# Decoder on one core: weights, last norm and memory products between the first experts and the second self attention

## What is computed

```python
def _L0_ffn_ref(x, w_router, w_gate, w_up, w_down, ..., shared_w_gate, shared_w_up, shared_w_down):
    probs = softmax(xt @ w_router)                     # 128 experts, the 4 best
    basis = silu((xt @ w_gate).reshape(T, 8, 256)) * (xt @ w_up).reshape(T, 8, 256)
    ...
    shared = silu(xt @ shared_w_gate) * (xt @ shared_w_up) @ shared_w_down
    return out + shared
def _L1_attn_ref(x, Wq, Wk, Wv, memory, memory_norm, memory_weight):
    q, k, v = x @ Wq.T, x @ Wk.T, x @ Wv.T             # 4 queries x 8 heads x 16
    probs = softmax(einsum('bsqhd,bthd->bqhst', qh, kh) * 0.25)
    a_dot = einsum('bqhst,bthd->bsqhd', probs, vh)
    sigma_q = elu(q.reshape(b, s, 4, 128))
    a_mem = sigma_q @ memory / (sigma_q @ memory_norm)
    w = sigmoid(memory_weight)
    return a_dot * (1 - w) + a_mem * w
...
x = layernorm(x + _L0_ffn_ref(x, ...))                 # third of six such steps
x = layernorm(x + _L1_attn_ref(x, ...))                # fourth
```

## Time and profile before

| what | us |
|---|---|
| median of 3 runs | 2482.82 |
| the three runs | 2481.49, 2482.82, 2499.75 |
| the execution that was profiled | 2499.76 |
| its span, first to last instruction | 2496.9 |
| end of the basis tiles to end of the experts' output products | 1427 to 1622 |
| PE idle between the experts and the first projection | 18.11 |
| self attention, from its first turn to its last product | 1623 to 1990 |

### The profile page before, as it was taken

How to read it: one execution, slowest core, us unless ns; L and a number is a source line. 1 busy time by engine, 2 the same in 40 slices (tenths; PEclk the granted TensorE clock), 3 DMA queues, 4 the chain that set the end, 5 groups by cost and what they waited for, 6 DMA issues and landing times. The chain is left out here.

```text
span 2496.9 us, 36997 instructions
## 1 busy us (share of the span) xinstructions
PE 2163.4 (87%) x13655; PEld 1731.6 (69%) x13669; DVE 1256.4 (50%) x3242; ACT 997.4 (40%) x2273; POOL 684.8 (27%) x627
## 2 busy tenths in 40 slices
PE   7999999999997889689999999858989748888774
PEld 6789889889875666568888777746555337766542
DVE  2654554553565666551111123246777546676646
ACT  3322232232235666431111111135656527777632
POOL 2732342332311111114343300035444222232110
PEclk9999999999996666899999999968999969999886
DMA  4210010100002100101000000033323030000001
GB/s 138 91 35 30 22 35 30 28 32 22 22 1 74 38 27 1 56 9 51 34 34 17 1 1 1 1 65 60 54 46 60 9 118 14 27 14 10 1 9 67
DMA packets 41297, 86.43 MB, mean 35 GB/s; under 512 B 6176, under 2 KB 20768, under 8 KB 38176
## 3 DMA queue, kind: packets, MB, share of 16 engines
q1 hardware_dynamic: 41120, 84.08, 12.0%
HBM read 63.55 MB, written 4.26 MB: 27 GB/s over the span
## 5 line engine op out<-in xcount | busy, mean ns | idle before, releaser
L1123 PE MATMUL PS<-WH,bXH 128*128 128x512 f32 x512 | 201.6, 394 | 5.4 <-POOL WL L1400 5.4
L1123 PE MATMUL PS<-WL,bXH 128*128 128x512 f32 x512 | 201.0, 393 | 0.0
L1123 PE MATMUL PS<-WH,bXL 128*128 128x512 f32 x512 | 200.9, 392 | 0.0
L1805 DVE TENSOR_REDUCE aM<-PS 128x4 f32<-128x1024 f32 x128 | 155.1, 1222 | 49.8 <-PE PS L1645 48.8
L1318 DVE SCALAR_TENSOR_TENSOR s<-s,cf,PS 128x256 f32<-128x256 f32 x112 | 53.9, 481 | 250.5 <-ACT s L1238 241.5
L1238 ACT ACTIVATE s<-PS 128x256 f32<-128x256 f32 x128 | 49.3, 385 | 280.1 <-PE PS L1123 280.1
L1748 ACT ACTIVATE aPT<-PS 128x1024 f32<-128x1024 f32 x128 | 129.5, 1024 | 70.2 <-PE PS L1665 69.2
L307 PE MATMUL PS<-aXH,QKH 128*128 128x512 f32 x384 | 154.0, 401 | 0.0
L307 PE MATMUL PS<-aXH,QKL 128*128 128x512 f32 x384 | 151.7, 395 | 0.0
L307 PE MATMUL PS<-aXL,QKH 128*128 128x512 f32 x384 | 151.5, 395 | 0.0
L506 ACT ACTIVATE sq<-PS 128x768 f32<-128x768 f32 x64 | 52.0, 812 | 209.0 <-PE PS L397 163.4
(11 more groups left out here) (400 smaller groups left out, 6161.0 us busy)
## 6 DMA issues: line engine op xcount, KB each, us to landing
lgB<-gate_sums SPq DMA_DIRECT2D x32, 256.0 KB, 3.7
sg<-in_gu SPq DMA_DIRECT2D x8, 1024.0 KB, 4.7
aqs<-aQH SPq DMA_DIRECT2D x64, 128.0 KB, 4.2
gQK<-in_Wqk SPq DMA_DIRECT2D x8, 768.0 KB, 5.9
xN<-in_xT SPq DMA_DIRECT2D x4, 1024.0 KB, 12.0
gC<-in_Wc SPq DMA_DIRECT2D x8, 512.0 KB, 4.9
xN<-in_x SPq DMA_DIRECT2D x4, 1024.0 KB, 7.1
cst<-in_cT SPq DMA_DIRECT2D x8, 512.0 KB, 4.7
```

The lines of the kernel that those rows point to most:

```text
L1123: mm = e.matmul(PS[:, b, :], x[:, kc, 128 * t:128 * t + 128], w[:, kc, :], start=kc == 0 and i == 0, stop=kc == KC - 1 and i == 2)
L1805: e.tensor_reduce(M[j % 2][:, :, :].rearrange("x q (h c) -> x h q c", h=2)[:, :, :, i], PS[:, b:b + 2, :].rearrange("p h (q k) -> p h q k" ...
```

## The change

In `experts0`: weight 9 is split in four chunks of its 512 rows, high half on ACT, low half on DVE in place of POOL, and PE waits chunk by chunk. Norms 0 to 2 are parted: statistics and seed after tiles 3, 7, 11; the other Newton rounds, the hand-over and ACT's part after tiles 4, 8, 12. Norm 3 leaves the stage.

In `attention1`: SP loads `aw` once weights 8 and 9 are split; the buffers are laid out in another order, so that `wst` lies where `sg` was. ACT splits to `WH` once PE has made the last shared products (`projected`), POOL in place of DVE splits to `WL`. `ks` is set to ones whole, one instruction for each buffer. The gates become a step `gate` at slot -27, norm 3 the steps `late1` to `late4` at slots -25 to -22. The step `memory` goes from 17 slots ahead of 8j to 11 for even j, from 22 to 18 for odd j.

```diff
@@ -1064,8 +1064,9 @@
+    up_hi, up_lo = K.flag("act_first_hi", KC), K.flag("dve_first_lo", KC)
...
-    w_hi, w_lo = K.flag("act_w_hi", 10), K.flag("pool_w_lo", 10)
+    w_hi, w_lo = K.flag("act_w_hi", 9), K.flag("pool_w_lo", 9)
@@ -1184,10 +1185,13 @@
             for a, k in ((0, 8), (1, 9)):
-                if t == 0:
+                if t == 0 and a == 0:
                     e.wait_ge(*w_hi.upto(k + 1))
...
                 for kc in range(KC):
+                    if t == 0 and a:
+                        e.wait_ge(*up_hi.upto(kc + 1))
+                        e.wait_ge(*up_lo.upto(kc + 1))
                     for i, (x, w) in enumerate(pair3((XH, WH[k % 2]), (XL, WL[k % 2]))):
@@ -1270,7 +1274,12 @@
                 silu(NT * k + t)
-            split_w(k + 2)
+            if k < 7:
+                split_w(k + 2)
+        e.wait_ge(*in_w[1].upto(5))
+        e.wait_ge(*t_mm.upto(8 * NT))
+        for kc in range(KC):
+            e.activation(WH[1][:, kc, :], sg[1][:, kc, :], ACTF.Copy).then_inc(up_hi.sem, 1)
@@ -1289,8 +1298,8 @@
                 shared(t + 1)
-            if t % 4 == 3:
-                norms[t // 4].apply_act(e)
+            if t >= 4 and t % 4 == 0:
+                norms[t // 4 - 1].apply_act(e)
@@ -1364,6 +1373,10 @@
             tile(n)
+        for kc in range(KC):
+            e.wait_ge(*up_hi.upto(kc + 1))
+            e.tensor_tensor(WL[1][:, kc, :], sg[1][:, kc, :], WH[1][:, kc, :].bitcast(F32),
+                            ALU.subtract).then_inc(up_lo.sem, 1)
@@ -1388,8 +1401,12 @@
             e.tensor_tensor(xN[:, t, :], PS[:, rooms["out", t][0], :], xN[:, t, :], ALU.add).then_inc(o_add.sem, 1)
-            if t % 4 == 3:
-                norms[t // 4].all_dve(e, step)
+            if t % 4 == 3 and t + 1 < NT:
+                norms[t // 4].stats(e, step)
+                norms[t // 4].seed(e, step)
+            elif t >= 4 and t % 4 == 0:
+                norms[t // 4 - 1].newton(e, step)
+                norms[t // 4 - 1].hand_over(e)
@@ -1440,7 +1458,8 @@
-    K.ends = (o_mm.upto(NT), u_hi.upto(2 * NT), o_add.upto(NT), t_add.upto(7 * NT), w_lo.upto(10))
+    K.late, K.loadable, K.projected = norms[NP - 1], (w_lo.upto(9), up_lo.upto(KC)), (h_mm.upto(NT),)
+    K.ends = (o_mm.upto(NT), u_hi.upto(2 * NT), o_add.upto(NT), t_add.upto(7 * NT), w_lo.upto(9), up_lo.upto(KC))
@@ -1451,11 +1470,10 @@
-    ends, came = K.ends, list(K.tx)
+    ends, came, late, loadable, projected = K.ends, list(K.tx), K.late, K.loadable, K.projected
...
-        PT = W("aPT", [128, 8, 2, 512])
@@ -1463,16 +1481,17 @@
+        M = [W(f"aM{i}", [128, 2, 16]) for i in range(2)]
+        rc, rm = W("arc", [128, 2, 16, 1]), W("arm", [128, 2, 2, 1])
+        mw, w1, w0 = W("amw", [128, 1]), W("aw1", [128, 1]), W("aw0", [128, 1])
+        mem = W("mem", [128, 130])
+        PT = W("aPT", [128, 8, 2, 512])
...
-        M = [W(f"aM{i}", [128, 2, 16]) for i in range(2)]
...
-        rc, rm = W("arc", [128, 2, 16, 1]), W("arm", [128, 2, 2, 1])
-        mem = W("mem", [128, 130])
-        mw, w1, w0 = W("amw", [128, 1]), W("aw1", [128, 1]), W("aw0", [128, 1])
@@ -1485,8 +1504,8 @@
         for lead, what, i in (((28, "turn_hi", 0), (27, "turn_lo", 0), (26, "key", 0), (25, "value", 0), (24, "query", 0),
-                               (23, "value_turn", 0), (22, "query", 1), (20, "elu", 0), (17, "memory", 0)) if j % 2 == 0 else
-                              ((28, "query", 0), (26, "query", 1), (24, "elu", 0), (22, "memory", 0))):
+                               (23, "value_turn", 0), (22, "query", 1), (20, "elu", 0), (11, "memory", 0)) if j % 2 == 0 else
+                              ((28, "query", 0), (26, "query", 1), (24, "elu", 0), (18, "memory", 0))):
             put(base - lead, 6, what, j, i)
@@ -1496,15 +1515,18 @@
+    put(-27, 7, "gate", 0)
+    for i, what in enumerate(("late1", "late2", "late3", "late4")):
+        put(-25 + i, 7, what, 0)
...
-    w_hi, w_lo = K.flag("act_w_hi", 11), K.flag("dve_w_lo", 11)
+    w_hi, w_lo = K.flag("act_w_hi", 11), K.flag("pool_w_lo", 11)
...
-    cleared, ones = K.flag("pool_cleared", 6), K.flag("pool_ones", 6)
+    cleared, ones = K.flag("pool_cleared", 6), K.flag("pool_ones", 3)
@@ -1690,13 +1712,13 @@
     def scalar(e):
-        for w in ends:
+        for w in projected:
             e.wait_ge(*w)
...
             e.activation(part(WH, m, h), source(m, h), ACTF.Copy).then_inc(w_hi.sem, 1)
-        e.wait_ge(*in_mw.upto(1))
-        e.activation(w1[:, :], mw[:, :], ACTF.Exp, scale=-1.0).then_inc(g_exp.sem, 1)
+        for w in ends:
+            e.wait_ge(*w)
         for what, j, i in plan:
@@ -1731,6 +1753,11 @@
                              ACTF.Identity, scale=w0[:, 0:1]).then_inc(v_out.sem, 1)
+            elif what == "gate":
+                e.wait_ge(*in_mw.upto(1))
+                e.activation(w1[:, :], mw[:, :], ACTF.Exp, scale=-1.0).then_inc(g_exp.sem, 1)
+            elif what == "late4":
+                late.apply_act(e)
             elif what == "elu":
@@ -1757,17 +1784,6 @@
         step = K.steps(e, "dve_step")
-        e.wait_ge(*in_w.upto(1))
-        for n, (m, h) in enumerate(blocks):
-            e.wait_ge(*w_hi.upto(n + 1))
-            e.tensor_tensor(part(WL, m, h), source(m, h), part(WH, m, h).bitcast(F32), ALU.subtract).then_inc(w_lo.sem, 1)
-        e.wait_ge(*g_exp.upto(1))
-        step(e.tensor_scalar(w1[:, :], w1[:, :], 1.0, None, ALU.add))
-        e.reciprocal(w1[:, :], w1[:, :]).then_inc(g_out.sem, 1)
-        e.wait_ge(*g_out.upto(1))
-        e.tensor_scalar(w0[:, :], w1[:, :], -1.0, 1.0, ALU.mult, ALU.add).then_inc(g_out.sem, 1)
-        e.wait_ge(*in_mem.upto(3))
-        e.tensor_scalar(mem[:, 0:128], mem[:, 0:128], w1[:, 0:1], None, ALU.mult).then_inc(g_out.sem, 1)
         for what, j, i in plan:
@@ -1777,6 +1793,22 @@
                                 XH[x][:, :, :].bitcast(F32), ALU.subtract).then_inc(x_lo.sem, 1)
+            elif what == "gate":
+                e.wait_ge(*g_exp.upto(1))
+                step(e.tensor_scalar(w1[:, :], w1[:, :], 1.0, None, ALU.add))
+                e.reciprocal(w1[:, :], w1[:, :]).then_inc(g_out.sem, 1)
+                e.wait_ge(*g_out.upto(1))
+                e.tensor_scalar(w0[:, :], w1[:, :], -1.0, 1.0, ALU.mult, ALU.add).then_inc(g_out.sem, 1)
+                e.wait_ge(*in_mem.upto(3))
+                e.tensor_scalar(mem[:, 0:128], mem[:, 0:128], w1[:, 0:1], None, ALU.mult).then_inc(g_out.sem, 1)
+            elif what == "late1":
+                late.stats(e, step)
+            elif what == "late2":
+                late.seed(e, step)
+            elif what == "late3":
+                late.newton(e, step)
+            elif what == "late4":
+                late.hand_over(e)
             elif what == "key":
@@ -1833,16 +1865,23 @@
     def gpsimd(e):
+        for w in projected:
+            e.wait_ge(*w)
+        for n, (m, h) in enumerate(blocks):
+            e.wait_ge(*w_hi.upto(n + 1))
+            e.tensor_tensor(part(WL, m, h), source(m, h), part(WH, m, h).bitcast(F32), ALU.subtract).then_inc(w_lo.sem, 1)
         for w in ends:
             e.wait_ge(*w)
-        for y in range(3):
-            for h in (0, 1):
-                e.memset(ks[y][64 * h + 32:64 * h + 64, :, :].bitcast(F32), 1.0).then_inc(ones.sem, 1)
-                e.wait_ge(*ones.upto(2 * y + h + 1))
+
+        def clear(y):
+            e.memset(ks[y][:, :, :].bitcast(F32), 1.0).then_inc(ones.sem, 1)
             e.memset(V[y][:, :, :, 16:32], 0.0).then_inc(cleared.sem, 1)
...
             e.wait_ge(*cleared.upto(2 * y + 2))
+
+        for y in range(3):
+            clear(y)
         for what, j, i in plan:
@@ -1874,9 +1913,11 @@
     def sync(e):
+        for w in loadable:
+            e.wait_ge(*w)
+        e.dma_start(wst[:, :, :], d["aw"]).then_inc(in_w.sem, 16)
         for w in ends:
             e.wait_ge(*w)
-        e.dma_start(wst[:, :, :], d["aw"]).then_inc(in_w.sem, 16)
         e.dma_start(mw[:, :], d["memw"].rearrange("(a n) -> a n", a=1).broadcast_to([128, 1])).then_inc(in_mw.sem, 16)
@@ -1889,7 +1930,7 @@
-                    e.wait_ge(*ones.upto(2 * y + 2))
+                    e.wait_ge(*ones.upto(y + 1))
```

## The result

The changed kernel takes 2428.12 us (median of 4 runs, 2418.93 to 2448.20), the kernel before 2491.28 in the same measurement (4 runs, with the earlier ones, 2481.49 to 2507.09): ratio 0.9755, 95% interval 0.9712 to 0.9798, some 61 us less. The profiled execution has a span of 2431.2 us, against 2496.9.

What follows compares the result with a forecast made beforehand. TensorE was taken to bound the stages, the gain being its idle time and the low clock after holes. Terms -7 - 19 - 15.6 - 6 - 10 = -57.6 us took 2482.82 to 2425 us; range 2407 to 2451.

Steps and rivals of the forecast that it cites:

- Part 1: Experts stage, shared expert: splitting the last weight in chunks removes PE's 4.29 us hole and the slow matmuls after it, -7 us.
- Part 2: Experts stage: parting norms 0 to 2 shortens PE's waits before the output products to 0.7 us and avoids low clock, -19 us.
- rival 2: Norms and prologue: short waits still cost the clock, -11 in place of -19 and 5 us more; 2438 us, chance 0.12.
- Part 3: Handover to the self attention: early weights, splits beside matmuls and a later last norm bring the key product forward, -15.6 us.
- Rival 4: Handover: the earlier start does nothing, as gate's DMA or POOL's splits hold PE as long; 2447 us, chance 0.06.
- Part 4: Self attention's prologue: scores 0 no longer wait behind both memory products; second key product 21.6 us earlier, 6 from this part.
- Part 5: Self attention's steady part: moved memory products avoid waits for POOL's `sgm`, -1.8 us a period, taken as -10, ends -20 and +15.
- Rival 1: Steady part: DVE becomes the bound in slots 5 to 7, +15 in place of -10; 2450 us, chance 0.12.
- Rival 3: Self attention falls to the low clock, as four cross attention slices at 0.6 suggest; up to 2585 us, chance 0.04.
- The rule of the Trainium skill: Prologue: DVE's two-port mode and POOL exclude each other; late norm's two tensor-scalars could wait, making the sum 3 us smaller.

Runs made afterwards that it cites:

- e1: Changed kernel with the last shared weight split whole again, high half on ACT, low half on POOL; first turn of the self attention 6.1 us later.
- e3: Changed kernel with the load of the attention's weights issued at the end of the experts stage again; turn to key product 15.4 us against 3.7.
- e4: Changed kernel with the norm of group 3 whole at the end of the experts stage again; turn to key product 16.2 us against 3.7.
- e5: Changed kernel with the memory products back at their old slots, 17 (even j) and 22 (odd j); last turn back 20.0 us later.
- e7: Changed kernel with only the even memory product back at 17 slots ahead, the odd one left at 18; last turn back 4.0 us earlier.
- e11: Changed kernel with the even memory products back at 17 slots ahead, save for j = 0, which stays at 11; 2420.72 us, ratio 0.9720 to the kernel before.
- e12: As e11, and SP sends the rows of maxima ahead of the query stack for j = 0 alone; ratio 0.9738 to the kernel before.
- e9: Changed kernel with the odd memory product moved from 18 to 11 slots ahead, 8 slots from the even one; last turn back 18.3 us later.
- e8: Changed kernel with SP sending the rows of maxima of even j ahead of the query stack preceding them; ratio 0.9800 to the kernel before.
- e10: As e8, and the odd memory product at 11 slots ahead; ratio 0.9792 to the kernel before.

## Why the prediction was right, point by point

The forecast was -57.6 us by the sum, 2425; measured were -61 by the ratio and 2428.12, and -63 between the profiles from T0 to the end. That the absolute time is off by only 3 us is in part luck: 2425 rests on a median before of 2482.82, which with the fourth run is 2491.28, and from that the sum gives 2434.

*Part 1* (-7): -7.0 between the profiles, 6.1 when undone. Both halves of the argument, hole and clock, are shown by e1.

*Part 2* (-19): -18.4 and 17.1 when undone. The remaining wait of 0.7 one tile later was 0.6, three times. It did not lower the clock (4.37 for 18 products), so rival 2 fell here. Behind the longer holes of the prologue the clock did fall (0.55 from 1616 to 1620 us, 0.50 from 1643 to 1648), but as it did in the kernel before, and the 5 us that rival 2 added there did not come.

*Part 3* (-15.6): -15.5. The distance from ACT's `aXH` to the key product carried over nearly as it stood, 2.5 for 2.4. POOL's splits took 9.50 us, where I took 8.7 between 6.8 and 17; they ended 0.2 us after the key product began, and PE did not wait for them. That either of norm and load alone holds most of the handover is shown by e3 and e4. Of the 15.5, 1.5 is the gate's new place, which the forecast counted without naming it, as it put the new key product behind `aXH` alone. Rival 4 fell with this.

*Part 4* (-6, with scores 0 at -23.3 in all): scores 0 are 23.7 us earlier in distance from the turn (20.8 against 44.5), the second key product 22.9. What I took wrong: the gate's small load takes 6.6 us before because it stands behind the 1.5 MB of weights; without them it landed 2.5 us after its issue at 1595.02, so the gate did not hold the key's copy. That copy began 6.4 us after the turn, where the forecast had 8.1. Of these 1.7 us, 0.5 is seen at scores 0 (20.8 from the turn, 21.3 forecast) and 1.3 at the second key product (28.0, 29.3 forecast); the way from one to the other was not traced. The idle time for the query's low half stayed, as the sum said: 6.49 us.

*Part 5* (-10, bounds -20 to +15): -14.9. The mechanism was right for the odd product: e5, e7 and the end of `sgm` show what it waited for. It was wrong for the even one, which was to win 1.3 a period where it left and to cost no more where it came: e7, e11 and e12 put it back, and their last turn back is 4.0, 2.6 and 3.9 us earlier than the changed kernel's. The term was mis-sized because it left out the clock. At full clock the period went from 39.0 to 37.9, -1.1 where I had -1.8; the rest is that the kernel before loses 1 to 4 us in some periods at the lower clock (they are 41.8, 39.0, 42.8, 39.1 and 40.1) and the changed one mostly doesn't. I named that gain as the low end of a bound and gave it no place in the sum, and I had lowered -12.6 to -10 without a reason. So it is partly luck that -10 lies near -14.9: a gain per period set too high and a clock left out work against each other. The 0.4 us a period that PE was to stand behind DVE's `aXL` did not come, for PE doesn't wait for `aXL` in the steady part; 0.4 came at `aam`, as 2.0 us in five waits.

*Rival 1* (DVE the bound in slots 5 to 7) did not come: PE's waits for DVE in six periods were 16.4 us before (1720 to 1960 us) and 19.3 after (1660 to 1895), 3 more where the rival needed 12 to 21. e9 says how near it was: DVE's `aXL` holds PE by 1.6 a period as soon as one product fewer stands ahead of it. *Rival 3* (the self attention at the low clock) did not come; the mean clock of its steady part rose from 0.94 (1700 to 1960 us) to 0.97 (1648 to 1895). Of the four slices that it cites, the first has PE at 7 tenths, not 8 to 9.

The rule of the Trainium skill that I weighed ("SBUF — State Buffer", "Who interferes with whom") showed in other places than I named. The late norm's two tensor-scalars took 0.17 each and did not wait. The gate's scaling of `mem` took 0.89 us beside POOL's clears, where it was 0.28 in the kernel before, and one of the late norm's Newton steps 1.17 us beside POOL's subtraction, against 0.16. The second reads two operands in SBUF while POOL reads SBUF, a case that the page lists. PE waited for neither. Where it had been on the path is the kernel before: there the norm's two tensor-scalars lost 1.5 us of the handover beside POOL's clears, as e4 shows.

## What to carry to other kernels

When an engine idles at a stage boundary, list everything that stands there side by side: removing one of two that run in parallel wins at most their difference (2.4 of 15.5 us for the norm, nothing for the load), and the gain belongs to the pair. A product in an in-order queue should be placed where its input has just become ready, moved only where its wait was, and each of the moved steps tried alone; here one of two moves won the steady part and the other cost 0.6 us a period. Where a view names what a wait was for, compare the ends of all that the instruction needs with its start: here the one that ended 0.1 us before was not the one named. And what is won in a prologue is won only if the last mark moves too. An idle time of TensorE costs more than its length, as the products after it may run at half the clock.

## What the runs showed of the hardware that I had not expected

Short waits can lower the clock as well, and not each time. The hole of 1.90 us ahead of tile 15's output products was followed by 18 products in 4.3 to 4.4 us in nine profiles (4.36 before, 4.38 in the changed kernel), and by the same products in 5.94 to 5.98 in e3, e4, e9 and e11. What decides between the two stays open. The 33 waits of 0.6 us behind the parted norms, three in each of eleven profiles, were never followed by slow products. In e8 a wait of 1.4 us was followed by slow products. In the steady part, the kernels without waits of about 2 us (the changed kernel, e1 to e4, e7, e11 and e12) ran at least four of five periods at a clock of 1.00; those with them did so in two (before) and one (e5), and e8, e9 and e10, with waits of up to 1.6 us that the changed kernel doesn't have, in two, one and two. Whether the waits lower the clock there or something else does both was not tested.

A load of 0.5 KB issued right behind one of 1.5 MB took 6.6 us to land, and 2.5 in the changed kernel, where the large one is long done. e3, which puts the large load back in front of it, and e4, which doesn't, settle it: 6.8 and 2.5 us. Its time is then that of the queue ahead of it, and not its own.
